# First MLP's opening work placed into the last batch of the attention before it, with four smaller reorderings

## What is computed

```python
x = _L0_xattn_ref(x, ctx, mask0, ...)   # 32 heads of 8, 8 kv heads; softmax; projection; layer norm
x = _L1_xattn_ref(ctx, x, mask1, ...)   # 16 heads of 16 over 256 own + 64 context keys; then an MLP:
#   attn_out = attn_out @ out_w + out_b + residual
#   out = rmsnorm(attn_out, postnorm_w)
#   out = gelu(out @ mlp_w1 + mlp_b1) @ mlp_w2 + mlp_b2;  return out + residual
x = _L2_xattn_ref(x, ctx, ...)          # one head: x + alpha * softmax(q k^T / 16) v @ w_o
x = _L3_xattn_ref(x, ctx, ctx, ...)     # twice: x + attention(layer_norm(x)), 16 heads of 128; then
#   x + gelu(layer_norm(x) @ w_fc1 + b_fc1) @ w_fc2 + b_fc2
```

## Time and profile before

| | us |
|---|---|
| median of 3 runs | 1140.73 (1137.78 to 1142.59) |
| the profiled execution | 1142.25 |
| its span in the profile | 1140.5 |
| PE busy | 1055.3 (93%) |
| DVE busy | 735.3 (64%) |
| ACT busy | 600.8 (53%) |
| POOL busy | 453.9 (40%) |

### The profile page before, as it was taken

How to read it: one execution, slowest core, us unless ns; L and a number is a source line. 1 busy time by engine, 2 the same in 40 slices (tenths; PEclk the granted TensorE clock), 3 DMA queues, 4 the chain that set the end, 5 groups by cost and what they waited for, 6 DMA issues and landing times.

```text
span 1140.5 us, 18505 instructions
## 1 busy us (share of the span) xinstructions
PE 1055.3 (93%) x6532; PEld 769.3 (67%) x6532; DVE 735.3 (64%) x1491; ACT 600.8 (53%) x1109; POOL 453.9 (40%) x436
## 2 busy tenths in 40 slices
PE   6989878799999977999989999999999999998998
PEld 3767755456665545777768866666788666667887
DVE  4868851567777626155568977667588776674553
ACT  3667764166665555354558753233587532345643
POOL 2778775424431104111224424333444243446241
PEclk9989998799999998998999999999999999999999
DMA  8010006777776021100013220000132100000000
GB/s 300 3 29 2 2 3 105 116 103 103 106 107 93 3 75 37 65 2 1 19 40 95 89 65 1 1 0 1 57 93 94 74 1 1 1 1 1 20 28 28
DMA packets 37152, 55.95 MB, mean 49 GB/s; under 512 B 12550, under 2 KB 29510, under 8 KB 34758
## 3 DMA queue, kind: packets, MB, share of 16 engines
q1 hardware_dynamic: 34998, 54.25, 21.4%
q10 hardware_dynamic: 2064, 0.52, 0.2%
HBM read 45.34 MB, written 9.18 MB: 48 GB/s over the span
## 4 chain that ended last, share of the span: by engine, by line
PE 70%; DVE 9%; POOL 8%; issue 5%; ACT 5%; DMA 2%; SPq 1%; POOLq 0%; ACTq 0%; DVEq 0%
PE ps L1170 8%; PE ps L1056 7%; PE ps L953 7%; PE ps L1149 7%; PE ps L1023 5%; PE ps L848 4%; PE ps L1067 4%; PE ps L1077 4%; PE ps L751 4%; POOL p L2086 3%; PE ps L815 3%; PE ps L1024 2%; PE ps L829 2%; ACT pT L1213 2%; ACT p L1216 1%
## 5 line engine op out<-in xcount | busy, mean ns | idle before, releaser
L1213 ACT ACTIVATE pT<-ps 128x512 f32<-128x512 f32 (+1 forms) x144 | 74.1, 558 | 155.4 <-PE ps L1161 123.8
L1719 DVE TENSOR_REDUCE nm<-ps 128x1 f32<-128x320 f32 x256 | 114.5, 486 | 51.8 <-PE ps L815 49.0
L1170 PE MATMUL ps<-v,pT 128*128 128x256 f32 x512 | 121.1, 389 | 8.0 <-DVE xr L1979 4.4
L2270 POOL TENSOR_TENSOR pn<-p,sm 128x1024 f32<-128x1024 f32 x32 | 60.8, 1901 | 152.4 <-DVE sm L1974 152.4
L2225 POOL TENSOR_TENSOR wl<-bun_m,wh 128x512 fp32r<-128x512 f32 x64 | 80.5, 1261 | 100.5 <-ACT wh L1213 100.5
L1149 PE MATMUL ps<-g,cT 128*128 128x512 f32 x256 | 114.8, 592 | 0.0
L1170 PEld LDWEIGHTS ps<-v,pT 128*128 128x128 f32 x512 | 95.5, 192 | 26.9 <-ACT pT L1213 15.1
L1023 PE MATMUL ps<-wb,hid_high 128*128 128x512 f32 x256 | 98.8, 422 | 0.0
L1216 ACT ACTIVATE p<-p 128x1024 f32<-128x1024 f32 (+1 forms) x64 | 68.5, 1070 | 51.7 <-DVE p L1966 47.2
L1216 ACT ACTIVATE pT<-ps 128x512 f32<-128x512 f32 x160 | 85.3, 606 | 15.4 <-PE ps L829 15.2
L815 PE MATMUL ps<-ks,qs 97*128 97x320 bf16 x256 | 71.7, 312 | 13.2 <-DVE nm L1719 7.7
(11 more groups left out here) (228 smaller groups left out, 2650.0 us busy)
## 6 DMA issues: line engine op xcount, KB each, us to landing
bun_m<-in_heads SPq DMA_DIRECT2D x32, 515.0 KB, 3.5
ks<-k_parts SPq DMA_DIRECT2D x48, 160.0 KB
qs<-q_parts SPq DMA_DIRECT2D x48, 128.0 KB
q_parts<-qp SPq DMA_DIRECT2D x8, 384.0 KB, 8.6
k_parts<-kp SPq DMA_DIRECT2D x8, 384.0 KB, 7.3
w<-in_w SPq DMA_DIRECT2D x2, 1024.0 KB, 4.9
xr<-in_x SPq DMA_DIRECT2D x1, 2048.0 KB, 15.9
out<-xr SPq DMA_DIRECT2D x16, 128.0 KB, 1.7
```

Source lines behind the costliest of these rows:

```text
L1170: last = mm(o, pT3[half][:, n, :], v3[:, bass.ds(i, 1), 4 * half + n, :], start=half == 0 and n == 0, stop=half == 1 and n == 3)
L1213: return nc.scalar.activation(o, x, ACT.Identity, bias=bias, scale=scale)
L1719: v.tensor_reduce(nm1[i % 2][:, t, h:h + 1], ps[:, u % 2, 0:KEYS1], X, ALU.max, negate=True).then_inc(D1t["maxima"].sem, 1)
```

## The change

Five edits, all of order; no arithmetic is added or removed.

1. SP issues the mask `maski` after `alpha` and the two loads of rows, not before them.
2. PE makes `keys_ctx1` after the first two units of scores of batch 0, not before them. The wait for the values `v0` moves from the first `turn0` to the first `values0`.
3. Into the last batch's chain of the second attention go: on ACT `wa_high` 0 and 1 (behind the last `h`), and behind `t` the GELU of up products 0 and 1 and `wa_high` 2 and 3; on DVE `xp_high` and `wa_low` 0 ahead of `b0`, `wa_low` 1 behind `b1`, `wa_low` 2 and 3 behind `r`; on POOL `xp_low` ahead of the last root; on PE up product 0 behind `T`, 1 and 2 behind `J`, 3 behind the last `N`. The functions `mlp_up`, `mlp_turn`, `move2`, `mlp_down` and the like only move to an earlier place in the file, and the GELU's loop body becomes `mlp_hidden`.
4. In chunk 2 of the first MLP `head_columns` stands at h = 6 (first) and h = 4 (second), not at h = 2.
5. In the second attention's feed, DVE's `mlp_normed` stands behind `shifted`, PE's `mlp_turn` behind both halves of `rows_out`, and the high part of the last MLP's first input is made by ACT (behind the exponential) and not by DVE.

```diff
-            sp.dma_start(maski[:, :], io["mask1"].partition_broadcast(P)).then_inc(dma_mi, 16)
             sp.dma_start(alpha[:, :], io["alpha"].partition_broadcast(P)).then_inc(dma_rowv, 16)
...
             sp.dma_start(row3[:, :, :], io["rows"][len(ROWS) - 3:, :].partition_broadcast(P)).then_inc(dma_rowv, 16)
+            sp.dma_start(maski[:, :], io["mask1"].partition_broadcast(P)).then_inc(dma_mi, 16)
...
                     if i == 0:
                         values_all0()
-                        keys_ctx1()
                 elif step == "S":
                     scores0(i, k)
+                    if i == 0 and k == 1:
+                        keys_ctx1()
...
+                    if n == B and move == "T":
+                        mlp_up(0, m1, 0, 0)
+                    elif n == B and move == "J":
+                        mlp_up(0, m1, 0, 1)
+                        mlp_up(0, m1, 0, 2)
+                    elif n == B + 1 and move == "N":
+                        mlp_up(0, m1, 0, 3)
...
-            mlp_products(0, m1)
+            mlp_products(0, m1, 4)
...
                         rows_out(i, k, 0)
+                        rows_out(i, k, 1)
                         for move, tile in feed(a, i, k):
...
                                 mlp_turn(0, tile, bank=6)
-                        rows_out(i, k, 1)
...
+            def mlp_hidden(m, w, i, f, func):
+                wait(EM[m]["up"], i, f)
+                wait(DM[m]["h_low"], i, f - 2)
+                nc.scalar.activation(w["hf"][f % 2][:, :], ps[:, f % 2, :], func, bias=fvec(m, f)
+                                     ).then_inc(AM[m]["gelu"].sem, 1)
+                wait(EM[m]["down"], i, -1)
+                wait(AM[m]["gelu"], i, f)
+                copy(w["h"][0][:, f, :], w["hf"][f % 2][:, :]).then_inc(AM[m]["h_high"].sem, 1)
...
+                    if move == "h" and (i, k) == (B - 1, QUADS - 1):
+                        act.wait_ge(dma_m1, 32)
+                        mlp_weights(0, m1, 0)
+                        mlp_weights(0, m1, 1)
+                    elif n == B and move == "t":
+                        mlp_hidden(0, m1, 0, 0, ACT.Gelu_apprx_tanh)
+                        mlp_hidden(0, m1, 0, 1, ACT.Gelu_apprx_tanh)
+                        mlp_weights(0, m1, 2)
+                        mlp_weights(0, m1, 3)
...
-                            elif i == 2 and h == 2:
+                            elif i == 2 and h == 6 - t:
                                 head_columns(t // 2)
...
+                    if n == B and move == "b0":
+                        dve.wait_ge(E1["heads"].sem, E1["heads"].end(B))
+                        mlp_input_high(0, m1, 0)
+                        mlp_up_low(0, m1, 0)
...
+                    if n == B and move == "b1":
+                        mlp_up_low(0, m1, 1)
+                    elif n == B and move == "r":
+                        mlp_up_low(0, m1, 2)
+                        mlp_up_low(0, m1, 3)
...
-                        for move, t in feed(a, i, k):
-                            if move == "T":
-                                mlp_normed(0, t)
                         if k + 4 < left:
                             stats(i, k + 4)
                         if k + 2 < left:
                             shifted(i, k + 2)
+                        for move, t in feed(a, i, k):
+                            if move == "T":
+                                mlp_normed(0, t)
...
+                if n == B:
+                    mlp_input_low(0, m1, 0)
                 if in_range(n - 1):
                     root1(n - 1)
```

More of the change, by code:

```diff
@@ L786, in _ @@
                         wait(A1["k_ctx"], 0)
-                        pe.wait_ge(pdv.sem, pdv.now(0, "v0"))
                     turn0(i, k)
                 elif step == "V":
+                    if i == k == 0:
+                        pe.wait_ge(pdv.sem, pdv.now(0, "v0"))
                     values0(i, k)
@@ L1026, in mlp_down, with mlp_products @@
                             last.then_inc(EM[m]["down"].sem, 1)
-            def mlp_products(m, w):
+            def mlp_products(m, w, done=0):
                 for i in range(NCH):
-                    for f in range(FT):
+                    for f in range(0 if i else done, FT):
                         mlp_up(m, w, i, f)
@@ L1483, in context_high @@
                 copy(cp3[0][:, :, :], cT[:, :, :]).then_inc(AH["ctx_high"].sem, 1)
+            for n in SLOTS:
+                for move, i, k in slot(n):
+                    if move == "P":
+                        weights1(i, k)
+                    elif move == "h":
+                        heads1(i, k)
+                    elif move == "q":
+                        own1(i, "q", 7)
+                    elif move == "k":
+                        own1(i, "k", 6)
+                    elif move == "n":
+                        columns1("normed_turned", i, 7, lambda kt: nT[:, kt, i * S:(i + 1) * S], scale="L1_norm")
+                    elif move == "t":
+                        if i:
+                            wait(E1["projected"], i - 1)
+                        columns1("heads_turned", i, 6, lambda kt: aoT1[:, kt, :], bias="L1_bv")
+                    elif move == "w":
+                        if n == SLOTS[0]:
+                            for t in (D0t["normed"], G0s["rows"], E0["normed_turned"]):
+                                act.wait_ge(t.sem, t.end(B))
+                        values1(i)
+                    elif move == "m":
+                        maxima_high1(i)
+                    if move == "h" and (i, k) == (B - 1, QUADS - 1):
[7 more added lines that the diff above has]
+                        mlp_weights(0, m1, 3)
             act.wait_ge(E1["normed_turned"].sem, E1["normed_turned"].end(B))
             act.wait_ge(D1t["normed"].sem, D1t["normed"].end(B))
-            mlp_gelu(0, m1, dma_m1, ACT.Gelu_apprx_tanh)
+            mlp_gelu(0, m1, ACT.Gelu_apprx_tanh, 2)
             for h in range(TAIL2):
@@ L1580, in _ @@
                 attend(a)
-            mlp_gelu(1, m3, dma_m3, ACT.Gelu)
+            mlp_gelu(1, m3, ACT.Gelu)
         @block.vector
@@ L1822, in mlp_rows @@
                     dve.wait_ge(loaded, 32)
-                    mlp_input_high(m, w, 0)
-                    for n in range(4):
-                        mlp_up_low(m, w, n)
                     for n in range(4):
@@ L2229, in mlp_low @@
                 if m == 0:
-                    mlp_input_low(m, w, 0)
                     for n in range(4):
```

217 lines of the change are left out of this document (93 added, 124 removed).

## The result

| | before | changed |
|---|---|---|
| median of 20 runs, us | 1141.16 (1135.92 to 1147.16) | 1137.05 (1128.39 to 1140.73) |
| ratio, 95% interval | 1 | 0.9955 (0.9938 to 0.9972) |
| span of the profiled execution, us | 1140.5 | 1138.1 |

The change gains 0.45%, some 5 us (3.2 to 7.1 by the interval); 1131.0 was forecast, a gain of about 10. The profiled execution alone shows only 2.4 us.

A forecast was written before the change was run, and what follows sets the result against it. PE, busy 93% of the span, was taken as the bound, with gains only where it waits or runs at 1.2 GHz. Terms 1.7 + 1.3 + 4.5 + 3.0 = 10.5 gave 1130.2 to 1131.75, taken as 1131.0; range 1126 to 1137.

The forecast's parts named there:

- within 0.5%: Whole kernel: outcome band of no change told from 1140.73 by under some 5.7 us, down to 1135.0; chance 0.16.
- what it gains at the head it keeps: Start: DVE runs unbroken after the first scores, so the earlier first mask step lasts, -1.7 us.
- a short wait: Start: the mask lands last and its conversion on DVE moves up, so a wait was possible; no size given.
- The bound of -0.5: Start: smallest gain of the mask and key reordering, if POOL's second key split becomes the limit.
- the half-clock side: Last batch's chain: product 0 ahead of the projection runs at half clock, normed rows 3.4 later, gain 0.7 us.
- 5.6 - 3.4 = 2.2: Last batch's chain: 5.6 us saved between normed rows and product 4, less normed rows 3.4 later.
- 5.6 - 1.6 - 1.5 = 2.5: Last batch's chain, full clock: 5.6 saved, normed rows 1.6 later with projection 1.1 shorter, 1.5 clock charge; gain 2.5 us.
- Rival R3: Last batch's chain: product 4 stays tied to casts and `hid_low` 0, clock falls, gain 0: 1132.3 us; chance 0.20.
- The difference of 4.54: Chunk 2 against chunk 1, 34.00 - 29.46: 3.4 of clock and 1.1 of waiting, all to go by moving head columns.
- the bound: Feed: largest gain, -5.8 us, with all steps 8.56, tail 9.08 and no clock fall in the matmuls behind.
- R4: Feed: transpose behind both output halves holds the exponential, steps of 12.3 us, slower at 1147; chance 0.04.
- an unlucky R1: Chunk 2: the clock still falls, gain 1.2 and not 4.5: 1134.3 us, chance 0.14; unlucky end set the range's top.

The follow-up runs named there:

- edit4_alone: The kernel before with only chunk 2's head columns moved from h = 2 to h = 6 and h = 4: ratio 0.9968.
- edit3_undone: The changed kernel with the last batch's chain back in its old order, the other four edits kept: 1137.04 us, ratio 0.9933.
- edits12_alone: The kernel before with only the mask load put last and the context keys behind two units of scores: ratio 0.9992.
- late_only: The changed kernel with `wa_low` 0 behind `b1` and up product 0 behind the projection, casts left ahead of `hid_low` 0: 1136.05 us, ratio 0.9940.
- low_first_late: The changed kernel with each `wb` cast behind one low part, `wa_low` 0 behind `b1` and up product 0 behind the projection: 1131.51 us, ratio 0.9890.
- low_first_late_u4: Casts behind low parts, `wa_low` 0 and product 0 late, as in low_first_late, but chunk 2's head columns back at h = 2: 1132.53 us, ratio 0.9909.
- low_before_wb: The changed kernel with each of the four `wb` casts behind one low part of the hidden values: 1131.52 us, ratio 0.9912.
- edit3_alone: The kernel before with only the new order of the last batch's chain in the second attention: ratio 0.9991.
- edit5_alone: The kernel before with only the second attention's feed reordered and its high-part cast on ACT: ratio 0.9987.

## Why the prediction was right in sign and half in size

Forecast 1131.0, range 1126.0 to 1137.0; measured 1137.05, 0.05 above the upper edge. The forecast started from a median of 1140.73, the 20 runs have 1141.16; the measured ratio on 1140.73 gives 1135.6, inside the range. The gain is 0.45% and not 0.9%. The ratio lies in the band called "within 0.5%" (chance 0.16), though clear of 1. By term:

| | forecast | stages |
|---|---|---|
| edits 1, 2 | -1.7 | -1.4 at the first mask step, +0.7 at the ninth |
| edit 3 | -1.3 | -0.3 to +0.2, about 0 |
| edit 4 | -4.5 | -1.4 always, -4.5 in three of five: -3.3 |
| edit 5 | -3.0 | -3.3 |
| sum | -10.5 | -5.9 |

The measured ratio gives 3.2 to 7.1 us, which holds the right column's sum and not the left one's.

**Edits 1 and 2.** The first mask step came earlier as forecast (1.4 in the mean, 1.6 in the changed kernel's profile). The step that failed is "what it gains at the head it keeps", from DVE's unbroken chain in the earlier trace rows: the chain is broken at 36.4 us, where DVE waits 1.09 for PE's scores before the change as well, and PE loses the gain at half clock. The stall of the conversion (2.19 for 1.20 in the changed kernel) was named as a short wait and not priced. The bound of -0.5, taken from POOL's split, was nearer the result, but not for its reason: the split held no scores up in the profiles read.

**Edit 3.** The mechanism was as told to the row: stall of 2.73, `ao` 2.1 later, product 0 ahead of the projection, product 4 behind casts and `hid_low` 0, idle PE, half clock. On the half-clock side the terms were near: the residual 3.5 later (3.4 forecast), product 4 some 1.9 earlier (5.6 - 3.4 = 2.2), the clock 1.5 to 2.2 (1.5). What was wrong is the other side of the sum, 5.6 - 1.6 - 1.5 = 2.5, which pulled the term to -1.3: it credits edit 3 with a projection 1.1 shorter. The projection takes 1.99 without edit 3 as well (edit4_alone, edit3_undone); the 2.87 of the kernel before was one draw of the clock. The 1.66 lost behind an idle of 3.08, from which the 1.5 was taken, was a draw too: behind the same idle time edits12_alone and edit4_alone lost nothing. Rival R3, that edit 3 does nothing because product 4 is tied to the casts, is what happened.
The Trainium skill's rule on the port pair (SBUF — State Buffer, "Who interferes with whom") described the stall rightly: 2.73 beside `xp_low`, 0.68 without. What the stall alone costs the kernel no run shows: late_only and low_first_late took it off, but moved product 0 as well, and both changed the stage by 0.15 at most.

**Edit 4.** The difference of 4.54 was taken whole as the head columns' doing. The runs split it: 1.42 (30.89 to 29.47) always, idle PE of 2.10 against 0.80; and 3.1 of clock, which came in three of the five profiles with that idle time and in none of nine without. The share of three in five is rough, from five profiles. I had read one execution's clock as the kernel's.

**Edit 5.** Right in both parts: steps 35.5 (35.9 forecast), last scores to last `pn` 9.54 (9.3). The 5.38 of the 16 matmuls behind it, counted only in the bound, was a draw of the clock in the old order (3.69 in edits12_alone and edit4_alone), and the new order has it too, one tile later, in low_first_late_u4. From the last `pn` to the end it is 106.2 to 106.6 us in the old order and 106.0 to 106.5 in the new (107.7 in that one): edit 5 gives nothing there. R4 did not come: the steps were 8.55, 9.21, 9.21 and 8.56, the wait of the transpose 0.46 at most.

**Luck.** No error balanced another: edits 1 and 2 were taken 2.4 too large, edit 3 1.3, edit 4 1.2. That the time still lies at the range's edge is owed to the width of the range, which was drawn up to "an unlucky R1", and not to the terms.

**A faster version.** The changed kernel with the casts behind the low parts (low_before_wb, low_first_late) is at 1131.5, ratio 0.9890 (0.9859 to 0.9921) for the second; against the changed kernel's 0.9955 that is 5 to 7 us, the 7.6 of stage C less some scatter.

## What to carry to other kernels

When work is moved ahead to fill an idle engine, follow the queue to the first item that was *not* moved and ask what it waits for: here four casts ahead of one subtraction made the whole edit worth nothing, and moving them behind it made it worth 6.5 us. A lowered clock in one profile is a draw, not a property: price the idle time that invites it, and take the clock's part with the share of profiles that show it. A head start counts only where the engine that bounds the stage still has it at a later mark: look there, and in several profiles.

## What was unexpected of the hardware

Programs with the same order in chunk 2, on the same chip, lose 3.1 us there or lose none, at the same 2.10 of idle PE (34.0 in edit3_alone, 30.9 in edit5_alone). The same holds for the 16 matmuls behind an idle of 3.08 at the end of the last attention: 5.38 in two profiles of the old order, 3.69 in two others. In the first attention the spread between profiles is 9 us (131.9 to 140.6), the largest of the five stages; PEclk drops to 0.50 in it at other places each time. The idle stretch of 5.43 us ahead of product 4 was followed by half clock both times, for 5.6 us in the changed kernel and 3.9 in edit3_alone. Why the clock falls at one idle stretch and not at another of the same length stays open: no run here controls it. A smaller thing: the int32 conversion of the mask on DVE took 0.42 in edit5_alone, where POOL's `tc` had all but ended, and 2.19 in the changed kernel, where it ran beside it.
